# Sums of squares on VectorE, and another order of weight transposes and first ternary products in a one-core transformer block

## What is computed

```python
x2 = _ln(x) * (1.0 + scale2) + shift2
h = jax.nn.gelu(x2 @ ffn_w1 + ffn_b1, approximate=False)
x = x + gate2 * (h @ ffn_w2 + ffn_b2)          # x3 below
...
w1 = _ternary_weight(W_fc, GROUP)              # -1, 0, 1 times a scale per 64
h = jnp.einsum('bsd,hd->bsh', x, w1)
h = jnp.square(jax.nn.relu(h))
hn = _rms_norm(h)                              # over the 1024 hidden features
w2 = _ternary_weight(W_proj, GROUP)
out = x_in + jnp.einsum('bsh,dh->bsd', hn, w2)
```

## Time and the profile before

| | us |
|---|---|
| median of 3 runs (lowest, highest) | 374.98 (374.57, 375.18) |
| the profiled execution | 375.05 |
| its span, first to last instruction | 373.2 |
| VectorE busy, share of the span | 222.2, 60% |
| TensorE busy, share of the span | 350.4, 94% |
| mean granted clock of TensorE, share of full speed | 0.987 |

### The profile page before, as it was taken

The page is one execution under the profiler, slowest core; times in us unless marked ns, Lnnn a source line. Parts: engine busy times, 40 slices in busy tenths (PEclk is TensorE's granted clock), DMA queues, the critical chain, the costliest instruction groups (busy, mean ns, idle before and its releaser), DMA issues.

```text
span 373.2 us, 5718 instructions
## 1 busy us (share of the span) xinstructions
PE 350.4 (94%) x1968; PEld 302.5 (81%) x1968; DVE 222.2 (60%) x388; ACT 197.7 (53%) x516; POOL 128.4 (34%) x111
## 2 busy tenths in 40 slices
PE   2799999999999999999999999999899999995974
PEld 2789889888888888988888888888778787885863
DVE  5772337436536643543753644477888648796694
ACT  1554664545455654456555456555667456663741
POOL 2532323322723242442432164443541200261461
PEclk9999999999999999999999999999999999997998
DMA  7923031000302100023000020010000000000002
GB/s 242 367 72 113 1 114 56 2 0 2 113 15 98 56 0 0 23 90 112 0 0 0 0 112 1 2 56 3 0 2 1 0 2 0 2 0 0 1 30 84
DMA packets 11777, 16.52 MB, mean 44 GB/s; under 512 B 672, under 2 KB 7920, under 8 KB 11760
## 3 DMA queue, kind: packets, MB, share of 16 engines
q1 hardware_dynamic: 11760, 16.30, 13.0%
HBM read 15.25 MB, written 1.05 MB: 44 GB/s over the span
## 4 chain that ended last, share of the span: by engine, by line
PE 79%; DVE 10%; ACT 3%; issue 2%; DMA 2%; SPq 1%; POOL 1%; DVEq 0%; ACTq 0%
PE bank L938 18%; PE bank L940 18%; PE bank L939 18%; PE bank L965 8%; PE bank L984 7%; PE bank L973 4%; DVE hbuf L882 3%; DMA t_up<-in_L_cond_ffn_b_dram 2%; DVE hid_lo L682 2%; PE bank L1198 2%; PE bank L1208 1%; DVE raw_qk L653 1%; DVE w_lo L682 1%; PE bank L1052 1%; PE bank L1061 1%
## 5 line engine op out<-in xcount | busy, mean ns | idle before, releaser
L339 POOL TENSOR_TENSOR prob<-prob,rinv 128x512 f32<-128x512 f32 x32 | 33.3, 1041 | 149.8 <-DVE rinv L761 149.8
L484 ACT ACTIVATE prob<-bank,nbias 128x128 f32<-128x128 f32 x128 | 45.2, 365 | 39.1 <-DVE nbias L755 39.1
L752 DVE TENSOR_REDUCE negmax<-bank 128x4 f32<-128x512 f32 x32 | 22.1, 691 | 73.5 <-PE bank L965 73.5
L938 PE MATMUL bank<-x_hi,wqk_hi 128*128 128x512 f32 x128 | 53.8, 420 | 0.0
L940 PE MATMUL bank<-x_hi,wqk_lo 128*128 128x512 f32 x128 | 50.6, 395 | 0.0
L939 PE MATMUL bank<-x_lo,wqk_hi 128*128 128x512 f32 x128 | 50.3, 393 | 0.0
L455 ACT ACTIVATE o_hi<-bank,bias 128x512 fp32r<-128x512 f32 x32 | 22.0, 687 | 39.6 <-PE bank L984 39.6
L459 ACT ACTIVATE vals<-bank 128x512 f32<-128x512 f32 x32 | 19.1, 597 | 36.4 <-PE bank L940 36.4
L411 POOL TENSOR_TENSOR raw_qk<-raw_qk 128x512 f32<-128x512 f32 x13 | 18.4, 1415 | 51.9 <-ACT raw_qk L609 51.6
L984 PEld LDWEIGHTS bank<-probT,vals 128*128 128x128 f32 x256 | 33.3, 191 | 3.4 <-DVE probT L686 0.6
L690 DVE TENSOR_SCALAR kT<-bank,bias 128x512 f32<-128x512 f32 x32 | 24.0, 749 | 19.4 <-PE bank L940 19.4
(11 more groups left out here) (148 smaller groups left out, 802.8 us busy)
## 6 DMA issues: line engine op xcount, KB each, us to landing
raw_qk<-in_L_cond_qkv_w_dram SPq DMA_DIRECT2D x8, 512.0 KB, 4.7
raw_v<-in_L_cond_qkv_w_dram SPq DMA_DIRECT2D x4, 512.0 KB, 3.8
raw_o<-in_L_cond_out_w_dram SPq DMA_DIRECT2D x4, 512.0 KB, 3.5
xt<-in_x_dram SPq DMA_DIRECT2D x2, 512.0 KB, 4.6
xr<-in_L_cond_ada_w_dram SPq DMA_DIRECT2D x1, 1024.0 KB, 10.1
raw_w<-in_L_cond_ffn_w_dram SPq DMA_DIRECT2D x2, 512.0 KB, 7.6
t_raw<-in_L_ffn_W_fc_dram SPq DMA_DIRECT2D x4, 256.0 KB, 3.6
t_raw<-in_L_ffn_W_proj_dram SPq DMA_DIRECT2D x4, 256.0 KB, 3.8
```

The costliest lines, as they stand in the source:

```text
L339: nc.gpsimd.tensor_tensor(e, e, rinv[:, j % 2, :].unsqueeze(2).broadcast_to([P, SQ, P]), ALU.mult).then_inc(norm_done, 1)
L484: e = nc.scalar.activation(prob[:, j % 2, s, :], bank[BS][:, s * P:(s + 1) * P], ACT.Exp, bias=nbias[:, j % 2, s:s + 1], scale=SCALE, accu ...
L752: nc.vector.tensor_reduce(negmax[:, j % 2, :], bank[BS][:, :].rearrange("p (s t) -> p s t", s=SQ), axis=AX.X, op=ALU.max, negate=True).the ...
L938: nc.tensor.matmul(dst, ah, bh, start=start and n == 0, stop=False)
```

## The change

GpSimd no longer adds squares; VectorE does it for all chunks (`add_squares`). GpSimd makes the last ternary values before `rstd_of(3)`. The weight transposes move forward: `transpose_fc` behind the seventh block of `ffn1(0, .)`, `transpose_proj` amid `ffn2(0, 1)`, and VectorE's four copies with them. `normalise(3)` comes behind all of half 0's low parts. x3 of half 0 is made and rounded a step earlier. The first ternary products start behind the first chunk of `ffn2` of half 1, one between each two chunks, all of `ternary2(0, .)` comes ahead of half 1, and half 1's second products are in another order, with its sums of squares ahead of the last chunk's. The whole diff:

```diff
--- before.py
+++ after.py
@@ -395,22 +395,15 @@
             for j in range(2, UG):
                 unit(NG - 1, j, last=True)
             ternary_signs(NG - 1)
+            ternary_values(NG - 1)
             rstd_of(3)
-            ternary_values(NG - 1)
 
             def row_scale(quad):
                 q = slice(quad * SQ, (quad + 1) * SQ)
                 pool.wait_ge(ms_done, quad + 1)
                 nc.gpsimd.tensor_tensor(rms[:, q], ms[:, q], neg_half[:, :], ALU.pow).then_inc(rms_done, 1)
 
-            for quad in range(NQ):
-                for c in range(1, NC - quad):
-                    pool.wait_ge(sq_done, NC * quad + c + 1)
-                    if c > 1:
-                        pool.wait_ge(sq_sum, (NC - 1) * quad + c - 1)
-                    nc.gpsimd.tensor_tensor(h2_sum[:, quad, :], h2_sum[:, quad, :], h2[:, c % 2, :], ALU.add).then_inc(sq_sum, 1)
-                    if quad and c == 1:
-                        row_scale(0)
+            row_scale(0)
             row_scale(1)
             pool.wait_ge(scaled, 1)
             nc.gpsimd.tensor_tensor(xr[:, B - 1, :], h2[:, 1, 0:D], xt[:, B - 1, :], ALU.add).then_inc(last_done, 1)
@@ -584,7 +577,7 @@
             nc.scalar.activation(ones[:, :], neg_half[:, 0:2], ACT.Copy, scale=-2.0).then_inc(ones_set, 1)
             for c in range(NC):
                 ffn1_gelu(1, c)
-                if c == 4:
+                if c == 3:
                     x3_hi(0)
 
             def relu_of(quad, c):
@@ -594,15 +587,15 @@
                     act.wait_ge(r_done, n - 1)
                 nc.scalar.activation(relu[:, n % 2, :], bank[n % 2][:, :], ACT.Relu).then_inc(relu_done, 1)
 
-            def ternary_hidden(quad, c):
+            def ternary_hidden(quad, c, between=None):
                 n = NC * quad + c
                 act.wait_ge(r_done, n + 1)
                 hi_part(hidden(quad, c)[0], hbuf[:, n % 2, :], r_h)
+                if between:
+                    between()
                 if c:
-                    if c > 2:
-                        act.wait_ge(sq_sum, (NC - 1) * quad + c - 2)
-                    elif quad:
-                        act.wait_ge(sq_sum, (NC - 1) * quad)
+                    if c > 2 or quad:
+                        act.wait_ge(sq_sum, (NC - 1) * quad + max(c - 2, 0))
                     dst = h2[:, c % 2, :]
                 else:
                     dst = h2_sum[:, quad, :]
@@ -612,8 +605,7 @@
             for c in range(NC):
                 if c + 1 < NC:
                     relu_of(0, c + 1)
-                ternary_hidden(0, c)
-            x3_hi(1)
+                ternary_hidden(0, c, between=(lambda: x3_hi(1)) if c == NC - 1 else None)
             relu_of(1, 0)
             for c in range(NC):
                 if c + 1 < NC:
@@ -837,6 +829,11 @@
                     return step
                 return gate(0), gate(1), residual(0), residual(1)
 
+            def copy_wT(n):
+                dve.wait_ge(wt_mm, n + 1)
+                nc.vector.tensor_copy((w1T, w2T)[n // 2][:, n % 2 * HID:(n % 2 + 1) * HID],
+                                      bank[2 + n][:, :].bitcast(BF16)).then_inc((w1T_done, w2T_done)[n // 2], 1)
+
             for c in range(NC):
                 h_lo_part(0, c)
                 if c == 0:
@@ -846,29 +843,25 @@
                 if c == 4:
                     dve.wait_ge(xr_done, 2)
                     stats_of(3, xr)
-                if c == 6:
-                    normalise(3, xr)
+            normalise(3, xr)
+            copy_wT(0)
+            copy_wT(1)
             modulate(3, SHIFT2, SCALE2, bank[BO:BO + 2])
 
-            def copy_wT(n):
-                dve.wait_ge(wt_mm, n + 1)
-                nc.vector.tensor_copy((w1T, w2T)[n // 2][:, n % 2 * HID:(n % 2 + 1) * HID],
-                                      bank[2 + n][:, :].bitcast(BF16)).then_inc((w1T_done, w2T_done)[n // 2], 1)
-
+            copy_wT(2)
+            copy_wT(3)
             gate0, gate1, residual0, residual1 = x3_steps(0)
             for c in range(NC):
                 h_lo_part(1, c)
                 if c == 0:
                     gate0()
+                    gate1()
                 if c == 1:
-                    gate1()
+                    residual0()
                 if c == 2:
-                    residual0()
                     residual1()
-                if c == 5:
+                if c == 4:
                     split_lo(0, KD * 4)
-                if c in (4, 6):
-                    copy_wT(c // 2 - 2)
 
             def ternary_r(quad, c):
                 n = NC * quad + c
@@ -898,34 +891,42 @@
                 nc.vector.scalar_tensor_tensor(out=xr[:, b, :], in0=bank[Y3[b]][:, 0:D], scalar=rms[:, b:b + 1],
                                                in1=xt[:, b, :], op0=ALU.mult, op1=ALU.add).then_inc(fin, 1)
 
-            for n in range(2):
-                copy_wT(2 + n)
+            def add_squares(quad, c):
+                dve.wait_ge(sq_done, NC * quad + c + 1)
+                if c > 1:
+                    dve.wait_ge(sq_sum, (NC - 1) * quad + c - 1)
+                nc.vector.tensor_tensor(h2_sum[:, quad, :], h2_sum[:, quad, :], h2[:, c % 2, :], ALU.add).then_inc(sq_sum, 1)
+
             gate0, gate1, residual0, residual1 = x3_steps(1)
             for c in range(NC):
                 ternary_r(0, c)
+                if c == NC - 1:
+                    residual0()
+                    residual1()
+                if c == NC - 2:
+                    gate0()
                 if c:
-                    if c == NC - 1:
-                        gate0()
                     ternary_r_lo(0, c - 1)
-            gate1()
-            residual0()
-            residual1()
+                if c == NC - 2:
+                    gate1()
+                if 2 <= c < NC - 1:
+                    add_squares(0, c - 1)
             ternary_r_lo(0, NC - 1)
             split_lo(1, KD * 5)
+            add_squares(0, NC - 2)
+            add_squares(0, NC - 1)
             for c in range(NC):
                 ternary_r(1, c)
                 if c:
                     ternary_r_lo(1, c - 1)
-                if c == 2:
+                if c >= 2:
+                    add_squares(1, c - 1)
+                if c == 1:
                     mean_squares(0)
-                if c in (3, 4):
-                    finish(c - 3)
+                if c in (2, 3, 4, 5):
+                    finish(c - 2)
+            add_squares(1, NC - 1)
             ternary_r_lo(1, NC - 1)
-            dve.wait_ge(sq_done, 2 * NC)
-            dve.wait_ge(sq_sum, 2 * (NC - 1) - 1)
-            nc.vector.tensor_tensor(h2_sum[:, 1, :], h2_sum[:, 1, :], h2[:, 1, :], ALU.add).then_inc(sq_sum, 1)
-            finish(2)
-            finish(3)
             mean_squares(1)
             for b in (4, 5, 6):
                 finish(b)
@@ -1141,6 +1142,24 @@
                 for n in range(NC):
                     ffn2_chunk(quad, n, c)
 
+            fc = t_w[:, :, 0:PIECE].rearrange("p g (n d) -> p g n d", n=2)
+            proj = t_w[:, :, PIECE:2 * PIECE].rearrange("p g (m c) -> p g m c", m=2)
+
+            def transpose_fc(k):
+                dst = bank[2 + k][:, :].bitcast(BF16)
+                for c in range(NC):
+                    m = nc.tensor.transpose(dst[:, c * P:(c + 1) * P], fc[:, c // 2, c % 2, k * P:(k + 1) * P], ident_bf[:, :])
+                m.then_inc(wt_mm, 1)
+
+            def transpose_proj(half):
+                dst = bank[4 + half][:, :].bitcast(BF16)
+                for c in range(NC // 2):
+                    n = half * (NC // 2) + c
+                    for mm in range(KD):
+                        m = nc.tensor.transpose(dst[:, c * D + mm * P:c * D + (mm + 1) * P],
+                                                proj[:, n // 2, mm, (n % 2) * P:(n % 2 + 1) * P], ident_bf[:, :])
+                m.then_inc(wt_mm, 1)
+
             pe.wait_ge(xs_lo, 3 * KD)
             pe.wait_ge(w1_l, 4)
             for c in range(NC):
@@ -1149,44 +1168,29 @@
                     out_product(NG - 1, UG - 1)
                 if c == 4:
                     transpose_y(1)
+                if c == 6:
+                    pe.wait_ge(t_done, NG)
+                    pe.wait_ge(ident_set, 2)
+                    transpose_fc(0)
+                    transpose_fc(1)
             pe.wait_ge(w2_l, 4)
             pe.wait_ge(y_acc, NQ * NG + 1)
             ffn2(0, 0)
             pe.wait_ge(xr_done, 2)
             transpose_x(3, bank[BO:BO + 2])
+            pe.wait_ge(w1T_done, KD)
             transpose_xr(1, bank[2:4])
-            ffn2(0, 1)
+            for n in range(NC):
+                ffn2_chunk(0, n, 1)
+                if n == 4:
+                    pe.wait_ge(mod_a, 4)
+                    pe.wait_ge(mod_d, 4)
+                    transpose_proj(0)
+                    transpose_proj(1)
             pe.wait_ge(xs_lo, 4 * KD)
-
-
-            fc = t_w[:, :, 0:PIECE].rearrange("p g (n d) -> p g n d", n=2)
```

(106 more changed lines are left out.)

14 lines of the change are left out of this document (removed).

## The result

The changed kernel takes 366.68 us (366.18 to 367.08, 4 runs) against 374.77 (374.52 to 375.18, 4 runs): a ratio of 0.978, with a 95% interval of 0.9765 to 0.9795. It is faster by 8.1 us; 366.5 was forecast.

A forecast was written before the change was run, and what follows sets the result against it. TensorE sets the pace (busy 94%), with VectorE the bound where it stops. Mean at 358.95 against 367.78 (-8.8) gives span 364.4; with 1.85 outside it 366.25; plus 0.25 for handovers 366.5 us, range 364.6 to 370.8.

The forecast's parts named there:

- Part 1: `ternary_values` before `rstd_of(3)`: second gate multiplication held some 1.6 us, sixth FFN1 block +1.06; the 0.93 us stop goes, -1.1 us.
- Part 2: Weight transposes moved forward: same TensorE work, one fill less per pair, -0.15 us; no new waits.
- Part 3: `x3_hi(0)` one chunk earlier, no transposes between second-half FFN1 blocks: its roundings lose cover, block 6 waits, +0.6 us.
- T: Start of the first ternary product on TensorE, forecast at 315.9 us against 316.9 before.
- U: TensorE's entry into the second ternary half, forecast at T + 24.5 = 340.4 us.
- rival A: Margins of 0.1 to 0.35 us break, VectorE comes late, each us passed on: 368.5 to 370.5 us; chance 0.15.
- Part 5: Second half with additions on VectorE, now the bound: addition 7 ends at U+17.55, mean starts at U+18.55 = 358.95.
- rival C: VectorE's long instructions are not GpSimd's doing and stay long, additions come on top: 377.7 us; chance 0.05.
- rival B: Clock falls in the second half, TensorE having gaps from U+9 on: near 371.4 us; chance 0.07.
- The tail: From the mean to the end, unchanged at 5.42 us; only 8 products follow the sums of squares.
- Part 4: First ternary products amid the chunks: 24.5 us from T to U, margins 0.1 to 0.35; stops and slow clock gone.
- the check in part 5: Second half's 7.0 us gain checked: 5.5 collisions, 2.9 left-over, 2.6 slow clock go, 3.7 additions come, 7.3 in all.

The follow-up runs named there:

- Experiment 4: Changed kernel, but GpSimd starts the last ternary values only after VectorE's three low parts of the first GELU half: 365.73 us, ratio 0.9757.
- experiment 7: Changed kernel with the weight transposes and VectorE's copies of them put back between and behind the second half's FFN1 blocks: 366.84 us, ratio 0.9784.
- experiment 3: Changed kernel with six more GpSimd additions of 128x512 in the second half, on unused tiles, nobody waiting for them: 373.0 us, ratio 0.9954.
- experiment 9: Changed kernel with six extra GpSimd memsets of 128x512 in the second half, which read nothing: 367.02 us, ratio 0.9782.
- 10: Changed kernel with six extra GpSimd copies of a 128x512 tile in the second half, one read each: 369.3 us, ratio 0.985.
- experiment 1: Changed kernel, but GpSimd adds the squares again, all but the last of the second half: 370.31 us, ratio 0.9893.
- experiment 2: Kernel before with its order, only that VectorE adds all squares: 366.17 us, ratio 0.9769.
- Experiment 8: Kernel before with VectorE's additions, plus later last values ahead of rstd, `normalise(3)` behind all eight low parts, earlier last sums of squares: 364.24 us, ratio 0.9717.

## Why the prediction was right, and where not

The time and the sign were right, and so were most of the terms. Point by point, with the 0.53 us of the start taken off where absolute times are meant:

- *Part 1, values against gates.* The hold was 1.72 us for 1.6, and FFN1's sixth block came 1.16 us later behind the first block (283.72 - 273.43 = 10.29, before 9.13) for 1.06. The stop of 0.93 us went. Experiment 4 shows that the collision, and nothing else, was the cost: 1.0 us comes back. It stays 0.16 below the 1.16 of the block.
- *Part 2, transposes at nothing.* Right: experiment 7 moves them back, and the distance changes by 0.07 us.
- *Part 3, `x3_hi(0)`.* The stop before block 6 is there, 0.35 us at 311.30. That block's first product starts 0.74 us after the one ahead of it (310.56), where the usual distance is 0.23, so 0.5 for the forecast 0.6. But without it, in experiment 7, only 0.16 us come back at the first ternary product: the move of the transposes, with the cover that it takes from `x3_hi(0)`, costs less than the 0.45 us that parts 2 and 3 add up to.
- *T and U.* The first ternary product starts 42.13 us behind the first FFN1 block for 41.94, the first of the second half 66.58 for 66.44. The margins of 0.1 to 0.35 us held, so rival A did not come.
- *Part 5.* From U to the mean 18.94 us for 18.55. The excess is at the end: addition 7 ends at U+17.80 for 17.55, for the last two additions, one behind the other, take 1.48 us and not 1.22; and from there to the mean it is 1.14 us for 1.00, since the sums of squares take 1.07. All squares and low parts from T on took 0.68 to 0.69 us with no GpSimd addition beside them, so rival C falls, and experiments 3, 9 and 10 show the cause by itself. The clock did not fall while TensorE had work (rival B); it did in experiment 3, where TensorE waited 2.28, 1.46 and 1.67 us.
- *The tail.* 5.45 for 5.42.
- *Slips of little weight.* The sum names the 0.07 us by which the profiled run lay above the median and doesn't take them off. Rival B's 371.4 doesn't follow from its terms: 15.3 us from U+9 on put the mean 5.75 us later, which is 372.3.
- *What was luck.* By the distance the sum was 0.53 us short, 0.14 of it up to U and 0.39 in part 5. The 0.25 us added for handovers made up for half of that, and so the forecast is 0.2 us from the median. That mean and span of the profile agree to 0.1 us is its start, early by as much as the sum was short.

**What failed is the account of the order.** Part 4, on the new places of the first ternary products, says of the two stops and the slow clock that they "have no cause any more", without a word on which of the two edits takes the cause away, and the check in part 5 counts 2.9 us of TensorE's left-over and 2.6 of slow clock as gains beside the 5.5 of collisions. The four combinations show that these are not gains of the order that come on top:

| | GpSimd adds | VectorE adds |
|---|---|---|
| old order | 374.77 | 366.17 |
| new order | 370.31 | 366.68 |

With GpSimd's additions in place the new order is worth 4.5 us (4.0 by the ratios). Without them it is worth nothing: 0.5 us on the wrong side, inside the intervals. Who adds is worth 8.6 us in the old order and 3.6 in the new (8.7 and 4.2 by the ratios). So both remedies act on the same loss, the holds of the first half. The traces show how. With GpSimd's additions VectorE's instructions of the first ternary half are longer than alone by 6.5 us in all in the old order (before) and by 2.7 in the new (experiment 1), where four of the seven additions fall into VectorE's waits; in the second half it is 5.3 and 5.4. The additions on VectorE take away all of it. That it is the even spacing of the first ternary products which opens these waits is read from the traces and was not tested by itself. The sum came out since it was a replay of the whole new kernel and not a sum of shares; the shares of its check, read as causes, would have misled. The two stops came from the seven holds of the first half, and the slow clock behind them from the stops: in experiment 2, in the old order without the holds, 0.61 and 0.23 us of stops are left and the clock is 1.00.

Of the new order, three things were weighed singly: the place of the values costs 1.0 us, that of the two `finish` 0.6, that of the transposes nothing. Experiment 8 puts its sums of squares ahead of the last outputs into the old order, together with a better place for the values and for `normalise(3)`; the sums of squares are the only edit behind the start of the second half, where 0.78 us are gained. How the other 1.19 split between the values and `normalise(3)` was not measured, nor what the first ternary products amid the second product are worth by themselves.

The Trainium skill (Perfetto Trace Analysis, Optimizing Scalar/DVE Operations) warns that moving work between GpSimd and VectorE might not help. Here the move towards VectorE did: 13 additions more on it gave 8.6 us in experiment 2. The reason that the skill gives, a read port that the two share, fits experiments 3, 9 and 10, where only GpSimd's reading instructions held VectorE, and it speaks for this move and not against it.

## What to carry to other kernels

Where VectorE is the bound, look for its long instructions beside GpSimd's reading ones: GpSimd's work is then not free, and an addition that takes VectorE 0.61 us itself can cost it 1.1 us on GpSimd. Replay the whole new order with the durations of the profile to get a time, but don't read the shares of such a sum as causes; two edits that each fill or remove the same stop don't add up, and the four combinations are what shows it. A large reordering beside a small edit should be tried without the small edit, and the small edit without it.

## What the runs showed of the hardware that was not expected

- TensorE's clock did not fall behind every stop. Experiment 1 has stops of 0.51, 0.72 and 1.68 us and later 0.49, 0.60 and 1.31, and its mean clock is 0.997. Before had 1.84 and 2.06 us with 1.0 us of work between them: the clock was still 1.00 behind the first, and 0.50 from 340 us on, in the second. In experiment 3 a single stop of 2.28 us, with TensorE busy all the time for 6.8 us ahead of it, was enough: the clock is 0.50 from 350.4 to 353.6 us. It is 0.50 again from 364 us on, behind stops of 1.46 and 1.67. Which property of the stops decides is left open.
- GpSimd's memset of 128x512 takes 0.53 us each time, its copy 0.62 at least and up to 1.12, an addition 1.28 and up to 1.69. The longer ones start while a VectorE instruction is in work (the copy of 1.12 us at 348.40, 0.03 us behind a square), so GpSimd is held as well.
- The start of the first FFN1 block differs between profiles by up to 1.25 us (273.43 to 274.68) with the same code ahead of it. Single spans of these profiles can't be compared to better than that. The distance to the last mean can: 85.52 and 85.55 us in the changed kernel and in experiment 9.
